# An audio tower kernel on one core: norms of the expert stage moved from GpSimd to ScalarE, output halves evacuated by two engines, first loads split over two queues

## What is computed

```python
h = tok(x)                      # two 8-step recurrences per sample (up, down), 64 features
h = h + attn(layernorm(h))      # 8 heads, exp(-gamma * |q-k|^2) scores
h = h + ffn(layernorm(h))

def ffn(x):                     # 16 experts, top 2 of them per token, hidden width 128/16 = 8 x 16
    gate_logits = x @ gate_w + gate_b
    topk_vals, topk_idx = top_k(gate_logits, 2); topk_w = softmax(topk_vals)
    h = relu(einsum('bsd,edf->bsef', x, w1) + b1)
    expert_out = einsum('bsef,efd->bsed', h, w2) + b2
    y = x + sum over the two chosen experts of topk_w * expert_out
    return (y - mean(y)) / sqrt(var(y) + 1e-5) * gamma + beta
```

## Time and profile before

| | |
|---|---|
| median of 3 runs | 873.49 us (873.44 to 873.87) |
| the profiled execution's own time | 871.59 us |
| its span, first to last instruction | 869.0 us |
| granted TensorE clock, mean | 0.982 of full speed |
| busy, share of the span | PE 88%, PEld 50%, DVE 81%, ACT 57%, POOL 60% |
| one step of stage C in steady state | 19.12 us |

### The profile page before, as it was taken

One profiled execution on the slowest core, in us unless ns is written; L12 is line 12 of the kernel. 1 busy time (PEld: TensorE's weight loads), 2 busy tenths in 40 slices (PEclk: granted clock), 3 DMA queues, 4 the chain that ended last, 5 costly groups with the idle time before them and its releaser, 6 DMA issues.

```text
span 869.0 us, 16981 instructions
## 1 busy us (share of the span) xinstructions
PE 766.4 (88%) x5712; PEld 438.4 (50%) x5712; DVE 702.2 (81%) x1810; ACT 491.1 (57%) x913; POOL 519.9 (60%) x719
## 2 busy tenths in 40 slices
PE   1699979999999999999999999899889899998894
PEld 1234346666666666666666665344344344444341
DVE  5376768999999999999999998577787877777652
ACT  0365668877887887888788785232333333333221
POOL 7260255445445344454454452469999999999867
PEclk9999979999999999999999999899999999999997
DMA  4300021111221112211112210000000000000000
GB/s 113 136 16 2 1 49 38 36 38 38 49 50 27 39 35 50 50 41 33 38 38 50 49 33 18 1 2 7 8 7 8 7 7 14 7 8 7 8 7 18
DMA packets 22789, 25.71 MB, mean 30 GB/s; under 512 B 12816, under 2 KB 21648, under 8 KB 22576
## 3 DMA queue, kind: packets, MB, share of 16 engines
q1 hardware_dynamic: 22384, 23.85, 11.5%
q10 hardware_dynamic: 320, 0.79, 0.4%
HBM read 5.30 MB, written 2.43 MB: 9 GB/s over the span
## 4 chain that ended last, share of the span: by engine, by line
PE 43%; DVE 33%; POOL 11%; issue 5%; ACT 3%; DMA 2%; SPq 1%; another core or an unknown queue 1%; POOLq 0%; DVEq 0%; ACTq 0%
DVE prob L753 15%; DVE m L769 9%; PE bank L1034 6%; PE bank L962 6%; PE bank L1149 6%; PE bank L1169 6%; PE bank L1082 5%; POOL cxn L425 5%; PE bank L1058 3%; PE bank L1060 2%; DVE qk L763 2%; POOL gated L436 2%; DVE wtok L877 2%; POOL cinv L421 2%; PE bank L1160 2%
## 5 line engine op out<-in xcount | busy, mean ns | idle before, releaser
L753 DVE TENSOR_SCALAR prob<-prob,cap_hi,cap_lo 125x250 f32<-125x250 f32 x512 | 232.7, 502 | 18.6 <-ACT prob L531 15.8
L401 POOL TENSOR_TENSOR sq<-sq 125x256 f32<-125x256 f32 x128 | 96.3, 759 | 170.7 <-ACT sq L545 126.7
L884 DVE SCALAR_TENSOR_TENSOR gated<-bank,nb,wb 128x500 f32<-128x500 f32 x160 | 115.7, 732 | 71.7 <-PE bank L1149 66.4
L1169 PE MATMUL bank<-gated,w_sb 64*64 64x500 f32 x1024 | 172.8, 594 | 0.0
L1149 PE MATMUL bank<-cs,w_sb 64*64 64x500 f32 x1024 | 170.4, 587 | 0.4 <-DVE gated L884 0.4
L531 ACT ACTIVATE prob<-bank 125x500 f32<-125x500 f32 x256 | 148.6, 591 | 38.0 <-PE bank L1060 35.0
L602 ACT ACTIVATE relu<-bank,b_sb 128x500 f32<-128x500 f32 x96 | 65.0, 678 | 175.1 <-PE bank L1149 170.5
L436 POOL TENSOR_TENSOR gated<-relu,wb 128x500 f32<-128x500 f32 x96 | 125.0, 1307 | 48.0 <-ACT relu L602 48.0
L1034 PE MATMUL bank<-prob,u 125*64 125x250 f32 x1024 | 125.8, 382 | 1.5
L1058 PE MATMUL bank<-m,s 128*125 128x500 f32 x256 | 111.0, 434 | 6.1 <-issue 6.1
L1060 PE MATMUL bank<-m,s 112*125 112x500 f32 x256 | 101.0, 395 | 0.0
(11 more groups left out here) (165 smaller groups left out, 1371.8 us busy)
## 6 DMA issues: line engine op xcount, KB each, us to landing
m<-m SPq DMA_DIRECT2D x128, 125.0 KB, 2.3
out<-res SPq DMA_DIRECT2D x16, 125.0 KB
xa<-xparts SPq DMA_DIRECT2D x4, 281.2 KB
w_sb<-in_w SPq DMA_DIRECT2D x1, 1024.0 KB
xw<-xparts SPq DMA_DIRECT2D x4, 140.6 KB
w_sb<-in_w SPq DMA_DIRECT2D x1, 512.0 KB
m<-s SPq DMA_DIRECT2D x32, 15.6 KB
xparts<-x_part SPq DMA_DIRECT2D x1, 375.0 KB, 4.0
```

Of the source, the lines that this page charges most:

```text
L753: last = dve.tensor_scalar(part, part, cap_hi[0:T, h:h + 1], cap_lo[0:T, h:h + 1], ALU.min, ALU.max)
L884: dve.scalar_tensor_tensor(gated[g % 8][:, :], up_bank(g)[:, 0:C], nb1[:, g:g + 1], wb[q % 2][:, :], ALU.max, ALU.mult).then_inc(c_gated, 1)
L1169: last = pe.matmul(y[cols, 0:C], w2_sb[rows, g, :], gated[g % 8][rows, :], start=g == 1 and rows is HI, stop=v == 7, skip_group_check=True)
```

## The change

In stage C:

- The norms' multiplications (cxn, and the output's yz) go from POOL to ACT as activations with `scale` = inverse deviation and `bias` = -mean x inverse deviation. ACT does cxn of pair p+1 in slot 1 of step p (behind the relu of group 1) and yz of pair p-3 in slot 5.
- POOL computes both norms' scales together, on tiles [T, 2, CH], at the head of step p (c_scales: four instructions).
- c_stats and c_aggr run one pair further ahead, at g = 12 and 13 of the step before.
- Bank 1 is copied out by DVE (`upper`, y_high, at g = 6) beside ACT's y_low; the sum of the two is POOL's (c_total, behind the multiplication of group 6); `extra` on PE waits for the two copies and not for the sum.
- c_result on POOL keeps gamma, beta and residual, behind groups 9 and 12.

At the start:

- SP issues x_in alone; A_LOADS go to ACT's queue, ahead of its wait for x_in, and an activation ahead of that wait loads ACT's table.
- The four rows of ones are all set by POOL, and only `replicate` waits for them, not the write of xparts.
- The partition order of the replicated rows changes (each source row three times in succession), and the weights' rows with it.

```diff
@@ sync
             sp.dma_start(x_in[:, :, :], xin[:, :, :]).then_inc(a_xin, 16)
-            for dst, src in A_LOADS:
-                sp.dma_start(full(dst), full(src)).then_inc(ld_a, 16)
-
             sp.wait_ge(a_split, SPLIT)
-            sp.wait_ge(s_prepg, PREP_GX)
             sp.dma_start(xparts.rearrange("r p (q l) -> q r p l", q=128), x_part[:, :, :, :]).then_inc(a_scr, 16)
             sp.wait_ge(a_scr, 16)
+            sp.wait_ge(s_prepg, PREP_GX)
...
-                             src.unsqueeze(0).to_broadcast([PARTS, PARTS * D_IN, n * C])).then_inc(s, 16)
+                             src.unsqueeze(1).to_broadcast([PARTS * D_IN, PARTS, n * C])).then_inc(s, 16)
@@ gpsimd
-            done(gp.memset(xa[32:64, :].bitcast(F32), ONES2))
-            done(gp.memset(xw[32:64, :].bitcast(F32), ONES2))
+            for rows in (slice(32, 64), slice(96, 128)):
+                done(gp.memset(xa[rows, :].bitcast(F32), ONES2))
+                done(gp.memset(xw[rows, :].bitcast(F32), ONES2))
...
+            def c_scales(q):
+                if valid(q):
+                    gp.wait_ge(c_ln, 2 * q + 2)
+                if valid(q - 4):
+                    gp.wait_ge(c_fin, 2 * (q - 4) + 2)
+                wait(gp, c_hn, min(q, PAIRS))
+                wait(gp, c_yz, q - 4)
+                gp.tensor_scalar(cneg[:, :, :], cagg[:, :, :, 0], -1.0, None, ALU.mult)
+                gp.tensor_tensor(cvar[:, :, :], cagg[:, :, :, 1], eps2[:, :, :], ALU.add).then_inc(c_inv, 1)
+                gp.wait_ge(c_inv, 3 * q + 1)
+                gp.tensor_tensor(cinv[:, :, :], cvar[:, :, :], mhalf2[:, :, :], ALU.pow).then_inc(c_inv, 1)
+                gp.wait_ge(c_inv, 3 * q + 2)
+                gp.tensor_tensor(cnb[:, :, :], cneg[:, :, :], cinv[:, :, :], ALU.mult).then_inc(c_inv, 1)
...
+            def c_total(q):
+                gp.wait_ge(c_yl, q + 1)
+                gp.wait_ge(c_yh, q + 1)
+                wait(gp, c_f, q)
+                gp.tensor_tensor(y_moe[:, :], y_low[:, :], y_high[:, :], ALU.add).then_inc(c_y, 1)
...
             def step_c(p):
+                c_scales(p + 1)
                 for n, g in enumerate(ACT_GROUPS):
                     if valid(p - 1):
                         gate_group(p - 1, g)
-                    if n == 0 and valid(p + 1):
-                        c_normed(p + 1)
-                    if n in (1, 3) and valid(p - 3):
-                        c_result(p - 3, n // 2)
+                    if n == 2 and valid(p - 2):
+                        c_total(p - 2)
+                    if n in (3, 4) and valid(p - 3):
+                        c_result(p - 3, n - 3)
@@ scalar
+            for dst, src in A_LOADS:
+                act.dma_start(full(dst), full(src)).then_inc(ld_a, 16)
+            act.wait_ge(a_table, 1)
+            act.activation(spare2[:, :], spare[:, :], ACT.Relu)
             act.wait_ge(a_xin, 16)
...
+            def normed(q):
+                act.wait_ge(c_inv, 3 * q + 3)
+                wait(act, c_xt, q)
+                for c in range(CH):
+                    last = act.activation(cxn[:, c, :, :], h_all[:, q * CH + c, :].unsqueeze(1).to_broadcast([T, 2, D]),
+                                          ACT.Identity, bias=cnb[:, 0, c:c + 1], scale=cinv[:, 0, c:c + 1])
+                last.then_inc(c_hn, 1)
+            def result(q):
+                act.wait_ge(c_inv, 3 * (q + 4) + 3)
+                wait(act, c_gres, 2 * q - 1)
+                for c in range(CH):
+                    last = act.activation(yz[:, 0, c, :], yt[:, c, :], ACT.Identity, bias=cnb[:, 1, c:c + 1],
+                                          scale=cinv[:, 1, c:c + 1])
+                last.then_inc(c_yz, 1)
...
+                if v == 1 and valid(p + 1):
+                    normed(p + 1)
+                if v == 5 and valid(p - 3):
+                    result(p - 3)
@@ vector
-            dve.memset(xa[96:128, :].bitcast(F32), ONES2)
-            dve.memset(xw[96:128, :].bitcast(F32), ONES2)
+            dve.memset(spare[:, :], 0.0).then_inc(a_table, 1)
...
-            def total(q):
-                dve.wait_ge(c_yl, q + 1)
-                wait(dve, c_f, q)
-                dve.tensor_tensor(y_moe[:, :], bank[1][:, 0:C], y_low[:, :], ALU.add).then_inc(c_y, 1)
+            def upper(q):
+                dve.wait_ge(c_dn, 8 * q + 8)
+                wait(dve, c_y, q)
+                dve.tensor_copy(y_high[:, :], bank[1][:, 0:C]).then_inc(c_yh, 1)
...
-                if valid(p + 1) and g == 0:
-                    c_stats(p + 1)
-                if valid(p + 1) and g == 1:
-                    c_aggr(p + 1)
+                if valid(p + 2) and g == 12:
+                    c_stats(p + 2)
+                if valid(p + 2) and g == 13:
+                    c_aggr(p + 2)
@@ tensor
             def extra(q):
-                wait(pe, c_y, q)
+                wait(pe, c_yl, q)
+                wait(pe, c_yh, q)
```

More of the change, by code:

```diff
@@ L58, in constants @@
         for part in range(1, PARTS):
-            rows = slice(half + part * PARTS * D_IN, half + (part + 1) * PARTS * D_IN)
+            rows = slice(half + part, half + XROWS, PARTS)
             for r in (rows, half + XROWS + part):
@@ L326, in _ @@
             done(gp.memset(mhalf[:, :], -0.5))
+            done(gp.memset(eps2[:, :, :], EPS))
+            done(gp.memset(mhalf2[:, :, :], -0.5))
+            done(gp.memset(cagg[:, :, :, :], 1.0))
             done(gp.memset(qkw[:, :, ONE_ROW:ONE_ROW + 2], 1.0))
@@ L414, in _ @@
             steps(step_b)
[L417 to L420, removed]
-                gp.tensor_tensor(cinv[:, :], cvar[:, :], mhalf[:, :], ALU.pow).then_inc(c_inv, 1)
-                gp.wait_ge(c_inv, 2 * q + 2)
-                wait(gp, c_xt, q)
-                for c in range(CH):
-                    last = gp.tensor_scalar(cxn[:, c, :, :],
-                                            h_all[:, q * CH + c, :].unsqueeze(1).to_broadcast([T, 2, D]), aggr[:, c, 0:1], cinv[:, c:c + 1],
-                                            ALU.subtract, ALU.mult)
-                last.then_inc(c_hn, 1)
+            def c_scales(q):
[11 more added lines that the diff above has]
+                gp.tensor_tensor(cnb[:, :, :], cneg[:, :, :], cinv[:, :, :], ALU.mult).then_inc(c_inv, 1)
             def gate_group(q, g):
@@ L620, in _ @@
             slot_c(0, 7)
-            for p in range(1, PAIRS + 2):
+            for p in range(1, PAIRS + 3):
                 for v in range(8):
@@ L816, in c_aggr @@
                 dve.wait_ge(c_ln, 2 * q + 1)
-                wait(dve, c_hn, q)
+                wait(dve, c_inv, 3 * q)
                 for c in range(CH):
-                    last = dve.bn_aggr(aggr[:, c, :], stats[:, c, :])
+                    last = dve.bn_aggr(cagg[:, 0, c, :], stats[:, c, :])
                 last.then_inc(c_ln, 1)
@@ L900, in result @@
                 for c in range(CH):
-                    last = dve.bn_aggr(aggr2[:, c, :], stats2[:, c, :])
+                    last = dve.bn_aggr(cagg[:, 1, c, :], stats2[:, c, :])
                 last.then_inc(c_fin, 1)
```

49 lines of the change are left out of this document (24 added, 25 removed).

## The result

The change makes the kernel faster by a little: median 867.67 us (four runs, 866.81 to 868.95) against 873.47 (four runs, 871.88 to 873.87), a ratio of 0.9938, interval 0.992 to 0.9957. The forecast was 914 with a range from 885 to 935. It was wrong in its sign, and the time lies outside its range.

A forecast was written before the change was run, and what follows sets the result against it. PE was taken as the bound, busy 17.12 of a 19.12 us steady step. Thirteen steady steps +42.7, first and last full steps +1.2, start -3.5: +40.4 on 871.59 is 912.0, and 1.9 to the median gives 914; range 885 to 935.

The forecast's parts named there:

- Part 1: Steady step of stage C: with cxn off POOL, PE's transposes don't wait; `extra` at +8.00 instead of +8.24, 0.2 us at best.
- Part 2: Steady step: POOL, free earlier, multiplies groups 4 and 6 against DVE's gate steps; `extra` at +9.57, 1.33 later than before.
- The faster rival: POOL's multiplications miss the two-input gate steps, if group 4 starts behind about +7.2, or hold nothing new: 855 us, chance 0.13.
- Part 3: From `extra` to the wtok transposes: POOL's group 9 and the gamma product hold DVE's gate steps, +0.63 at wtok.
- The remaining 3.96: Last stretch of a stage C step, from the wtok transposes to the next step: 3.96 us, as before the change.
- Part 4: PE idles 2.67 us ahead of `extra` in every step, so the clock falls in most, ten of thirteen, costing 1.7 each.
- Part 5: Start of the kernel: earlier split and replicate bring xa sooner, -3.5 us, bounds 0 and -6; new row order costed at nothing.
- the parts nearly cancel: Rival for stage C: `extra` at +8.5, wtok as before, 19.4 us a step, no change in total, 874; chance 0.05.

The follow-up runs named there:

- the expert stage alone: The changed kernel with the start's edits undone, the order of the replicated rows too: 879.31 us, ratio 1.0086 against the kernel before.
- two moves: The changed kernel with ACT's norm of pair 0 ahead of stage B's output copy and, in the first step, pair 1's behind group 4's relu: 863.21 us.

## Why the prediction was wrong, step by step

**Part 1, the scales: the mechanism right, the size wrong, and the choice between the ends unsafe.** "On 8 it costs between 1.03 and twice that. I take 1.03" was the step that decided. It measured 1.67, or 0.16 for each column beyond four. The reason given, that such an instruction is mostly fixed cost, does not hold for the power. ACT's four activations took 1.65 for an estimated 1.5, and the norm ended at +5.48, between my +4.8 and +7.0. "ACT is idle 3.14 there before the relu at +4.91, which hides it" was false: the norm ended 0.57 behind the time the relu was due, the relu came 0.48 late, and POOL with it.

**Part 2, POOL free at the wrong time: right as a mechanism, not met in the steady steps.** The sentence that failed is "If the scales take 2.06, group 1 delays the chain instead and group 4 the second step: the same within 0.3". I had two values for a price and treated the outcome as the same at both, without writing the chain down for a value between them (no run has the scales at 2.06). At 1.67 group 4 starts at +6.12, 0.45 behind L887, and falls between two gate steps that have two inputs. The faster rival named this place and put its threshold at +7.2; passing L887 and L890 was enough for most of it. Three traces show the mechanism where group 4 is on time: the power on four columns has `extra` at +9.42, the norm one slot later at +9.04 and the change's own last full step at +9.42, for a forecast of +9.57. The forecast of 21.08 for a step whose clock holds stands against 20.80 in the first of them.

**Part 3, behind `extra`: right.** From `extra` to the wtok transposes took 7.42, forecast 7.55; L896 took 1.15 (forecast 1.15) and the later steps were free, but for 0.64 on L900. The remaining 3.96 came as said. The sum with the real `extra` is 8.21 + 7.42 + 3.96 = 19.59, the measured step.

**Part 4, the clock: not tested at its premise in the steady steps, and too pessimistic where it was.** With 1.15 of idle time ahead of `extra` the clock held in every steady step of the change. With 2.35, nearest to the forecast's 2.67, it fell in two of thirteen, not ten, and a fall cost 1.5, not 1.7; the run of that kernel at 893.7 would have eight by the estimate above. The step that failed is "So I expect the fall in most steps", drawn from two steps in which PE had waited and the clock fell. Waits of that length do not settle it: seven of the traces have a last full step with a wait of 2.92, and the clock fell in two of them (the change, and the change with the old rows, 22.50 and 22.22) and held in five (20.80 or 20.81).

**Part 5, the start: one edit costed at nothing was the largest term of all.** "The new order of rows I cost at nothing" failed, with bounds given for it in the same breath (-6, "faster reads"). Alone it takes 7.6 us off the kernel before. The split came earlier as forecast (its first cast at 3.82, the replication issued at 12.12 for a forecast of 11.3). That was worth 4.4 us where the order was the old one (874.87 against the expert stage alone), near the forecast's 3.5, and nothing measurable on top of the new order in the kernel before (0.9929 against 0.992). The Trainium skill's rule on outermost dimensions, named above, bore on this edit and was not weighed.

**What no part held: the hand-over.** I read steady steps, first step and last step, and not the 25 us in which stage B ends while stage C's norms already run. Moving the norm to ACT put it in one queue with stage B's copies and exponentials; it cost 5.3 us, 2.10 of waiting and the fall of the clock behind it, and 4.5 came back with two moves. The first step of stage C I had put at a loss of 0.6; it gained 4.9 (15.81 for 20.70), since its wait for cxn and the fall behind it went, and no wait of over 2 us took their place.

**The account** in the two profiled executions: start -9.1 by the last unit of stage B, hand-over +5.3, first step -4.9, the steps from there to the last fold +6.4 (twelve times 0.46, the last full step's 0.3 and 0.6 behind it); that is -2.3 at the last fold and -2.5 in the span. Of the 43 us between this and the forecast's +40.4, 37 are the steady steps (forecast +42.7, measured +5.5). The rival that was nearest was "the parts nearly cancel" (its `extra` at +8.5, 19.4 a step, 874), to which I gave 0.05. Its step is nearly the measured one. That its total is only 6 us off is in part luck, since it held neither the row order (-7.6) nor the hand-over (+5.3) nor the first step (-4.9).

## What to carry to other kernels

When an operation leaves a busy engine, ask to the tenth of a microsecond when that engine takes its next work, and against what it then runs: here 0.46 us in the start of one POOL instruction was worth 1.2 us in each of thirteen steps, and less work was slower. Where a price has two ends, write the chain out at a value between them before calling the outcome the same. In a DMA that replicates, put the source's rows outermost and not the few copies, and follow a moved operation into the step where two stages overlap, not only into the steady one.

## What the runs showed of the hardware that was not expected

- **A replicating DMA and its order.** The same bytes into as many rows were used 11.3 us behind the issue with the three copies outermost, 7.0 with the 12 source rows outermost; the busy shares near the end were 0.21 and 0.88, the latter with other loads beside. SP's own issues behind it were short too (gw_sb 0.57 for 3.57).
- **POOL's power is not of fixed cost**: 1.03 on 4 columns, 1.67 on 8, in 125 partitions, while its other operations on those 8 columns took 0.20 to 0.23.
- **What a POOL instruction holds on DVE depends on its kind.** Under its multiplications of 500 columns a gate step with two SBUF inputs took 1.30, and a TENSOR_SCALAR on 4 columns, which has one, 1.15 for 0.17; under POOL's cxn (a TENSOR_SCALAR) L857 took 0.23. The Trainium skill, SBUF — State Buffer, section Who interferes with whom, has the first as a rule. By it the last would be held too, since POOL reads h_all from SBUF there; the trace disagrees.
- **Equal steps, unequal clocks.** The same 2.35 us of wait ahead of `extra` brought the granted clock of the step down to 0.92 in two of thirteen steps and left it at 1.00 in the rest. The same 2.92 did so in two of seven last full steps. The same 2.10 at the hand-over brought 0.50 over four us in the changed kernel and 1.00 with the norm one slot later. What decides between them is open here.
